# Squares of six blocks added by accumulating DMAs before TensorE sums them over the channels

## The chip, the cores and the metric

The kernel runs on one core of one Trainium2 chip. The metric is the device time of one execution in microseconds (us). Before the change it is 4678.69 us, the median of three runs (4672.37 to 4686.97).

## The reference, cut to what matters

Two layers work on x of shape (4, 1024, 1024). Each first forms a two-sided decayed sum over the sequence from the side tensor and gates it (`_bi_wkv`). The first layer ends in a linear map; the second ends in a root-mean-square norm, a router with top-4 of 32 experts, the experts, and a shared expert. The part that the change touches is the norm:

```python
def _rmsnorm(x, w, eps=EPS):
    var = jnp.mean(jnp.square(x.astype(jnp.float32)), axis=-1, keepdims=True)
    return (x * lax.rsqrt(var + eps)).astype(x.dtype) * w
...
h = _rmsnorm(x, norm_w)
flat = h.reshape(-1, H)
```

The mean of squares goes over the 1024 channels of each token.

## The kernel before, in words

Activations lie channel by channel: 128 channels on the partitions, tokens along the free axis. So there are CB = 8 blocks of 128 channels, and the 4096 tokens are worked on in HALVES = 8 halves of HALF = 512 tokens.

The program has three stages. In the first (units 0 to 7, up to about 330 us) VectorE (DVE), ScalarE (ACT) and GpSimd (POOL) compute the decayed sums of the first eight units alone, while TensorE (PE) helps to split weights. In the second (about 330 to 2000 us) each half has 32 steps. A step on PE is one `product` (L1457): 24 matmuls of 128x512. Steps 0 to 15 are the linear map of this half (`STEP_L`) and the shared expert's down product of the half before (`STEP_D`); steps 16 to 31 are gate and up products. Beside them halves 0 to 5 compute four more units each (`unit`, eight `fill` calls a unit, so that unit number q of a half holds fills 8q to 8q+7); halves 6 and 7 have no units. In the third stage (from about 2000 us) the experts are worked through.

All engines are programmed in order, by hand. Each engine's code for step i of half h is its `fill(h, i, ...)`; PE's is in `half`. The tables at the head of the file say at which step something is done. What the change touches, all in the second stage:

- DVE forms `C1[o]` (L1291), the normed layer's input, block o = 0 to 7.
- ACT squares it into the tile `SQ` at fill `SQUARE_AT[o]` = 3, 4, 5, 7, 9, 11, 13, 13 (L785). `SQ` is one buffer, so each square waits until the one before has been summed (semaphore `sums`).
- PE adds each square over the channels by one float32 matmul with the matrix `ones` (L1467, `square_sums`) after step `SUM_AT[o]` = 5, 5, 6, 8, 10, 12, 13, 14, accumulating in `SUM_BANK`. The trace shows each as two records.
- At step 15 (`R_AT`) ACT takes Ln and Exp of the sum into the tile `R` (L793, L795); DVE refines it (`root`, L1253 to L1261) and scales the blocks with it (`normalize`, L1270). PE then turns them by token (`by_token`, L1477, L1479), which waits for DVE.

Around them on ACT: at the fills of a unit, `edges` (L680, L683) copies the last column of a forward scan, which DVE's backward scan (L975, L983) starts from; `euk`, `inverse` and `sigmoid` (L652 to L656) also feed DVE. In unit q = 0 of a half, square 1 (fill 4) stands on ACT directly ahead of `edges(1)`, behind the issue of the side tensor's load (L665). `out_copy` (L768) copies turned outputs of the half before into the tile `RS`, and waits for the last store from it, which SP issues (L468) behind its loads of weight pieces (L396), which wait for PE's products.

POOL has one instruction for each unit, `clip` (L595), which waits for the side tensor's load and gives ACT's `side_exp` its input. From half 6 on it writes the experts' lists.

Of the kernel before, what the change touches and what calls it, by code (L numbers as in the profile page):

```python
# [9 lines left out]
CB = CH // P  # L10
TOK = BATCH * SEQ
TT = TOK // P
BLOCKS = BATCH * CB
HALF = SEQ // 2
HT = HALF // P
HALVES = TOK // HALF
PIECE = CB * P
FILLS_PER_UNIT = 8
UNITS_PER_HALF = BLOCKS // HALVES
STEPS = FILLS_PER_UNIT * UNITS_PER_HALF  # L20

ROUTED_TILES = TOK * TOPK // P + EXPERTS
# [18 lines left out]
SQUARE_AT = (3, 4, 5, 7, 9, 11, 13, 13)  # L41
SUM_AT = (5, 5, 6, 8, 10, 12, 13, 14)
R_AT = 2 * CB - 1

# [46 lines left out]
def adaln_moe(nc, x_t, side_t, cond, w_all, u_all, lin_sb, norm_w, router_t, shared_w, expert_w, out):  # L91
# [12 lines left out]
    with ctx:  # L104
# [76 lines left out]
        ones = sb("ones", P)  # L181
# [21 lines left out]
        s = {}  # L203
        for name in (
            "k_in x_in ramp consts_in cond_in kc ek ekv euk h_fwd h_edge h_bwd h_all den g_ln g_inv nf n_edge nb "
            "wv_done num num_w newton1 newton2 sig_steps sig_x gated gated_raw ratio ratio_out gated_out "
            "split_hi split_lo split_pe chunk product read_out c_hi c_lo sig1_steps sig1 c1 z sq z_hi z_lo res "
            "z_tr logits sums z_copy z_out mean r_ln r_exp newton_r r_set l_copy l_tr l_acc silu_steps silu_sig "
            "a_hi_s a_lo_s o_tr o_copy o_out prep prep_act masks rt rt_act rt_mask rt_pe cnt_copy "
            "fill_set fill_out add_idx_set apart entry_ready listed_in slots_in cols_set w1_hi w1_lo w2_hi w2_lo w1_read w2_read "  # L210
            "rows_in row_idx_set x_tr x_hi x_lo silu_done act_done a_tr a_hi a_lo y_hi y_lo y_out zero_set "
            "zero_out"
        ).split():
            s[name] = sem(name)
# [39 lines left out]
        def final(h, which=HALVES - 1):  # L254
            return isinstance(h, int) and h == which


# [275 lines left out]
        def _(pool):  # L533
# [56 lines left out]
            def clip(u, par):  # L590
# [4 lines left out]
                pool.tensor_scalar(EK, side_of[par], 30.0, None, ALU.min).then_inc(s["kc"], 1)  # L595

            clip(0, 0)
            with pool.Fori(0, BLOCKS // 2) as v:
                clip(2 * v + 1, 1)
                clip(2 * v + 2, 0)  # L600
            pool.wait_ge(s["zero_set"], 1)
            pool.dma_start(out[TOK:TOK + P, :], SPARE).then_inc(s["y_out"], 16)
            pool.wait_ge(s["rt_mask"], 1)
            pool.iota(entry.rearrange("p (t k w) -> p t k w", k=TOPK, w=2)[:, :, :, 0],
# [35 lines left out]
        def _(sc):  # L640
# [134 lines left out]
            def fill(h, i, first, prev, next_):  # L775
                if prev and i == 0:
                    act_hi(h - 1, CB - 1)
                if not before_all(h):
                    for o in range(CB):
                        if prev and i == copy_step(o):  # L780
                            out_copy(h - 1, o)
                        if i == square_step(o):
                            sc.wait_ge(s["c1"], h * CB + (o + 1))
                            wait(sc, "sums", h * CB + o)
                            sc.activation(SQ, C1[o], ACT.Square).then_inc(s["sq"], 1)  # L785
                    for o in range(CB):
# [4 lines left out]
                    if i == R_AT:  # L791
                        sc.wait_ge(s["sums"], h * CB + CB)
                        sc.activation(R, SUM_BANK, ACT.Ln, bias=eps[:, :], scale=1.0 / CH).then_inc(s["r_ln"], 1)  # L793
# [617 lines left out]
        def _(pe):  # L1411
# [49 lines left out]
            def square_sums(h, o):  # L1461
                pe.wait_ge(s["sq"], h * CB + (o + 1))
                if o == 0:
                    wait(pe, "z_copy", h * CB)
                    if final(h):
                        pe.wait_ge(s["entry_ready"], 1)
                pe.matmul(SUM_BANK, ones[:, :], SQ, start=(o == 0), stop=(o == CB - 1)).then_inc(s["sums"], 1)  # L1467

# [218 lines left out]
```

## Time and profile before

| | before |
|---|---|
| median of the runs | 4678.69 us |
| profiled execution, its span | 4682.9 us |
| PE busy | 4475.7 us, 96% |
| DVE busy | 2567.2 us, 55% |
| ACT busy | 1789.8 us, 38% |
| POOL busy | 722.8 us, 15% |
| time before the experts (first two stages) | about 2000 us |

The profiled execution has no time of its own listed beside its span; the span is 4.2 us above the median and within the range of the runs. Busy time is the time in which an engine works on an instruction; shares are of the span. A number in brackets behind a timeline row is how long the engine stood idle before it, and what ended that.

### The profile page before, as it was taken

What the parts mean: (1) busy time and instruction counts of PE and PEld (TensorE: products, weight loads), DVE (VectorE), ACT (ScalarE), POOL (GpSimd) and SP (SyncE); (2) the same over time, 40 slices, a digit from 0 to 9 for tenths busy, and PEclk for the clock granted to TensorE, in tenths of its full rate; (3) what the DMA queues carried; (4) which work ended last, traced back from release to release, by engine and by line L of the source; (5) the groups of instructions that cost most, each with busy time, mean ns of one, the idle gap of its engine ahead of it and who ended that gap; (6) DMA issues with size and microseconds to landing.
All of it is one profiled execution on the core that took longest, in us unless ns stands there. A gap on an engine that the chain in (4) does not pass through costs nothing.

```text
span 4682.9 us, 60901 instructions
## 1 busy us (share of the span) xinstructions
PE 4475.7 (96%) x19862; PEld 3545.7 (76%) x19863; DVE 2567.2 (55%) x2765; ACT 1789.8 (38%) x2596; POOL 722.8 (15%) x934
## 2 busy tenths in 40 slices
PE   6777999999999999999999999999999999999998
PEld 2245877777777877878888888888888888888887
DVE  8999999999999653433233434444341253333432
ACT  5665555555555333232222323334231142222321
POOL 1000000000000017211111112112111121111111
PEclk8888999999999999999999999999999999999999
DMA  6675767767676766754344545555552254444543
GB/s 226 235 263 184 274 241 268 251 223 282 240 268 226 270 212 190 251 182 111 95 131 112 170 112 160 171 166 150 182 168 57 61 186 145 112 112 116 161 109 61
DMA packets 247928, 835.08 MB, mean 178 GB/s; under 512 B 28160, under 2 KB 61056, under 8 KB 222976
## 3 DMA queue, kind: packets, MB, share of 16 engines
q1 hardware_dynamic: 172944, 572.77, 34.5%
q0 software_dynamic: 47728, 160.07, 15.5%
q10 hardware_dynamic: 27136, 100.67, 5.8%
q8 instruction: 72, 1.18, 0.1%
q14 instruction: 48, 0.39, 0.0%
HBM read 652.40 MB, written 181.01 MB: 178 GB/s over the span
## 4 chain that ended last, share of the span: by engine, by line
PE 80%; DVE 10%; issue 4%; ACT 3%; DMA 2%; POOL 0%; ACTq 0%; DVEq 0%; POOLq 0%; SPq 0%
PE ps L1593 34%; PE ps L1457 22%; PE ps L1607 16%; PE ps L1526 3%; PE ps L1479 1%; PE ps L1582 1%; DVE work L969 1%; DVE work L975 1%; DMA work<-rows_dram,row_idx 1%; PE ps L1477 1%; PE ps L1467 1%; DVE work L996 1%; DVE work L998 1%; DVE work L972 1%; DVE work L1002 1%
## 5 line engine op out<-in xcount | busy, mean ns | idle before, releaser
L1593 PE MATMUL ps<-halves 128*128 128x512 f32 x7152 | 1698.6, 393 | 3.5 <-DVE halves L1356 2.8
L1593 PEld LDWEIGHTS ps<-halves 128*128 128x128 f32 x7152 | 1338.5, 189 | 279.9 <-DVE halves L1356 3.1
L1457 PE MATMUL ps<-halves 128*128 128x512 f32 x6144 | 1450.2, 395 | 13.7 <-issue 12.5
L1457 PEld LDWEIGHTS ps<-halves 128*128 128x128 f32 x6144 | 1154.1, 189 | 287.2 <-issue 47.8
L1607 PE MATMUL ps<-halves 128*128 128x512 f32 x3576 | 834.9, 389 | 1.3 <-DVE halves L1372 1.3
L1607 PEld LDWEIGHTS ps<-halves 128*128 128x128 f32 x3576 | 671.1, 188 | 140.9 <-DVE halves L1372 1.6
L1356 DVE TENSOR_TENSOR halves<-ps,halves 128x1024 fp32r<-128x1024 f32 x150 | 183.7, 1225 | 905.2 <-ACT halves L852 905.2
L1351 DVE TENSOR_TENSOR halves<-work,halves 128x1024 fp32r<-128x1024 f32 (+1 forms) x320 | 440.2, 1433 | 83.6 <-ACT halves L856 83.3
L852 ACT ACTIVATE halves<-ps 128x1024 fp32r<-128x1024 f32 x150 | 154.0, 1027 | 862.4 <-PE ps L1593 862.4
L576 POOL DMA_INDIRECT out<-work,add_idx x149 | 249.8, 1677 | 1417.3 <-DVE work L1378 1382.2
L856 ACT ACTIVATE halves<-work 128x1024 fp32r<-128x1024 f32 (+1 forms) x320 | 369.1, 1229 | 67.0 <-PE ps L1607 56.5
L1372 DVE TENSOR_TENSOR halves<-ps,halves 128x256 fp32r<-128x256 f32 x298 | 112.4, 419 | 491.7 <-ACT halves L884 491.7
L595 POOL TENSOR_SCALAR work<-work 128x1024 f32<-128x1024 f32 x33 | 106.5, 3226 | 1419.9 <-DMA work<-side_t 1419.9
L884 ACT ACTIVATE halves<-ps 128x256 fp32r<-128x256 f32 x298 | 98.5, 382 | 544.4 <-PE ps L1582 544.4
L1378 DVE TENSOR_SCALAR work<-ps,acc 128x512 f32<-128x512 f32 x149 | 111.6, 749 | 276.4 <-PE ps L1607 266.5
L890 ACT ACTIVATE work<-ps,acc 128x512 f32<-128x512 f32 x149 | 102.1, 685 | 408.5 <-PE ps L1607 388.5
L566 POOL DMA_INDIRECT work<-rows_dram,row_idx x151 | 152.5, 1010 | 123.4 <-POOL row_idx L562 69.0
L1526 PE MATMUL ps<-ident,work 128*128 128x128 f32 x1200 | 157.6, 275 | 12.4 <-DMA work<-rows_dram,row_idx 12.4
L975 DVE TENSOR_TENSOR_SCAN work<-decay,edge_in,work 128x1024 f32<-128x1024 f32 x64 | 154.2, 2409 | 14.2 <-ACT edge_in L680 14.2
L1435 PE MATMUL ps<-plain,ident 128*128 128x512 f32 x128 | 83.0, 736 | 73.6 <-ACT halves L735 73.6
L983 DVE TENSOR_TENSOR_SCAN work<-decay,edge_in,work 128x1024 f32<-128x1024 f32 x64 | 150.7, 2355 | 0.0
L1526 PEld LDWEIGHTS ps<-ident,work 128*128 128x128 f32 x1200 | 137.1, 142 | 13.4 <-DMA work<-rows_dram,row_idx 13.3
(186 smaller groups left out, 3674.4 us busy)
## 6 DMA issues: line engine op xcount, KB each, us to landing
halves<-split_dram SPq DMA_DIRECT2D x512, 512.0 KB, 5.6
work<-expert_w SPq DMA_DIRECT2D x192, 1024.0 KB, 5.5
split_dram<-halves ACTq DMA_DIRECT2D x32, 1024.0 KB, 4.9
plain<-shared_w SPq DMA_DIRECT2D x32, 512.0 KB, 3.2
gated_dram<-work ACTq DMA_DIRECT2D x32, 512.0 KB, 4.1
work<-side_t ACTq DMA_DIRECT2D x32, 512.0 KB, 5.6
work<-x_t ACTq DMA_DIRECT2D x32, 512.0 KB, 3.7
ratio_dram<-work ACTq DMA_DIRECT2D x32, 512.0 KB, 4.2
```

The costliest lines, as they stand in the source:

```text
L566: pool.indirect_dma_start(hx, None, rows_dram[:, :], bass.IndirectOffsetOnAxis(row_idx[:, :].bitcast(u32), 0)).then_inc(s["rows_in"], 16)
L576: pool.indirect_dma_start(out[:, :], bass.IndirectOffsetOnAxis(add_idx[:, :].bitcast(u32), 0), y, None, compute_op=ALU.add).then_inc(s["y_ ...
L852: sc.activation(xhi, ps_xt[:, :], ACT.Copy).then_inc(s["x_hi"], 1)
L856: sc.activation(whi[q][:, part], staged(q, part), ACT.Copy).then_inc(s["w1_hi" if q < 4 else "w2_hi"], 1)
L975: ve.tensor_tensor_scan(F[:, ::-1], d, F[:, ::-1], edge_in[:, 0:1], ALU.mult, ALU.add).then_inc(s["h_bwd"], 1)
L983: ve.tensor_tensor_scan(G[:, ::-1], d, G[:, ::-1], edge_in[:, 1:2], ALU.mult, ALU.add).then_inc(s["nb"], 1)
L1351: ve.tensor_tensor(wlo[q][:, part], staged(q, part), whi[q][:, part].bitcast(f32), ALU.subtract)\
L1356: ve.tensor_tensor(xlo, ps_xt[:, :], xhi.bitcast(f32), ALU.subtract).then_inc(s["x_lo"], 1)
L1457: last = pe.matmul(bank(k % 4), w, op[:, part], start=(c == 0 and w is w_hi and op is hi), stop=(c == CB - 1 and w is w_lo))
L1526: last = pe.transpose(ps_xt[:, c * P:(c + 1) * P], hx[:, c * P:(c + 1) * P], ident[:, :])
L1593: last = pe.matmul(ps_h[:, a * 512:a * 512 + 512], xp[:, xk * P:(xk + 1) * P], wp[:, rhs], start=(xk == 0 and xp is xhi and wp is whi[q]), ...
L1607: last = pe.matmul(ps_y[:, h * 512:h * 512 + 512], ap_[:, (q * 2 + k) * P:(q * 2 + k + 1) * P], wp[:, rhs:rhs + 512], start=(q == 0 and k ...
```

## The change

In halves 0 to 6 only block 0's square goes to another tile, `R`, which is free at that time. The squares of blocks 1 to 5 still go to `SQ`, and each is added to `R` by a DMA with an accumulate, which POOL issues (`fold_square`): SBUF to SBUF, 128 partitions of 2 KB. So ACT's square o (2 to 6) waits for the landing of DMA o-1 (semaphore `sq_folded`) in place of a matmul. PE sums `R` once, at o = 5 (after step 12), then squares 6 and 7: three matmuls with `ones` in place of eight. Half 7 is as before. POOL's loop over the units is written out from unit 8 on, with the DMAs between the clips.

```diff
+ALONE = 2 * UNITS_PER_HALF
...
+FOLDED = 6
...
+        def folded(h):
+
+            return not final(h)
+
+        def squares_used(h, o):
+
+            return h * (CB - FOLDED + 1) + (o + 1 if final(h) else o - FOLDED + 2)
...
+            def fold_square(h, o):
+
+                pool.wait_ge(s["sq"], h * CB + (o + 1))
+                pool.dma_start(R, SQ, accum_op=ALU.add).then_inc(s["sq_folded"], 16)
+
             clip(0, 0)
-            with pool.Fori(0, BLOCKS // 2) as v:
+            with pool.Fori(0, ALONE // 2) as v:
                 clip(2 * v + 1, 1)
                 clip(2 * v + 2, 0)
+            for h in range(HALVES - 2):
+                for q in range(UNITS_PER_HALF):
+                    u = ALONE + h * UNITS_PER_HALF + q
+                    if q == 0:
+                        fold_square(h, 1)
+                    if q == 1:
+                        fold_square(h, 4)
+                        fold_square(h, 5)
+                    clip(u + 1, (u + 1) % 2)
+                    if q == 0:
+                        fold_square(h, 2)
+                        fold_square(h, 3)
             pool.wait_ge(s["zero_set"], 1)
             pool.dma_start(out[TOK:TOK + P, :], SPARE).then_inc(s["y_out"], 16)
+            for o in range(1, FOLDED):
+                fold_square(HALVES - 2, o)
...
                             sc.wait_ge(s["c1"], h * CB + (o + 1))
-                            wait(sc, "sums", h * CB + o)
-                            sc.activation(SQ, C1[o], ACT.Square).then_inc(s["sq"], 1)
+                            if folded(h) and o == 0:
+                                wait(sc, "z", h * CB)
+                            elif folded(h) and o <= FOLDED:
+                                wait(sc, "sq_folded", 16 * (h * (FOLDED - 1) + (o - 1)))
+                            else:
+                                wait(sc, "sums", squares_used(h, o - 1))
+                            sc.activation(R if folded(h) and o == 0 else SQ, C1[o], ACT.Square).then_inc(s["sq"], 1)
...
             def square_sums(h, o):
-                pe.wait_ge(s["sq"], h * CB + (o + 1))
-                if o == 0:
+                first = FOLDED - 1 if folded(h) else 0
+                if o < first:
+                    return
+                if o == first:
                     wait(pe, "z_copy", h * CB)
                     if final(h):
                         pe.wait_ge(s["entry_ready"], 1)
-                pe.matmul(SUM_BANK, ones[:, :], SQ, start=(o == 0), stop=(o == CB - 1)).then_inc(s["sums"], 1)
+                if folded(h) and o == first:
+                    pe.wait_ge(s["sq_folded"], 16 * ((h + 1) * (FOLDED - 1)))
+                else:
+                    pe.wait_ge(s["sq"], h * CB + (o + 1))
+                pe.matmul(SUM_BANK, ones[:, :], R if folded(h) and o == first else SQ, start=(o == first), stop=(o == CB - 1))\
+                    .then_inc(s["sums"], 1)
```

PE, in the loop over the halves, at the end of steps 5 and 6. Before:

```order
L1457 MATMUL ps<-halves 128x512 x11
L1467 MATMUL ps<-work,ones 128x512 [waits z_copy,sq]
L1490 REGISTER_ALU
L1493 MATMUL ps<-ident,work 128x128 [waits o_copy,read_out]
L1493 MATMUL ps<-ident,work 128x128 x3
L1467 MATMUL ps<-work,ones 128x512 [waits sq]
L238 REGISTER_ALU
L1457 MATMUL ps<-halves 128x512 [waits piece_in2_0,read_out]
```

Now (the changed file's L1491 is the product, L1534 the turning of outputs):

```order
L1491 MATMUL ps<-halves 128x512 x11
L1531 REGISTER_ALU
L1534 MATMUL ps<-ident,work 128x128 [waits o_copy,read_out]
L1534 MATMUL ps<-ident,work 128x128 x3
L240 REGISTER_ALU
L1491 MATMUL ps<-halves 128x512 [waits piece_in2_0,read_out]
```

Two sums and their waits for a square are gone here; the first sum now stands behind step 12 and waits for `sq_folded`.

ACT, in half 2, around fill 4 of its first unit (q = 0). Before:

```order
L665 DMA work<-side_t 128x1024 [waits gated]
L785 ACTIVATE work<-plain 128x512 [waits sums,c1]
L680 ACTIVATE edge_in<-work,edge 128x1 [waits h_fwd]
L683 ACTIVATE edge_in<-work,edge 128x1 [waits nf]
L691 ACTIVATE work<-work,uu 128x1024 [waits gated_raw]
L785 ACTIVATE work<-plain 128x512 [waits sums,c1]
```

Now:

```order
L694 DMA work<-side_t 128x1024 [waits gated]
L819 ACTIVATE work<-plain 128x512 [waits sq_folded,c1]
L709 ACTIVATE edge_in<-work,edge 128x1 [waits h_fwd]
L712 ACTIVATE edge_in<-work,edge 128x1 [waits nf]
L720 ACTIVATE work<-work,uu 128x1024 [waits gated_raw]
L819 ACTIVATE work<-plain 128x512 [waits sq_folded,c1]
```

The order is the same. The first of the two squares (block 1) now waits for the last DMA of the half before; the second (block 2) waits for the DMA of block 1.

POOL, in one half (h = 0 to 5) of the changed kernel, where before there were only the four clips (L605 now, L595 before):

```order
L610 DMA work<-work 128x512 [waits sq]
L605 TENSOR_SCALAR work<-work 128x1024 [waits ekv,k_in,h_fwd]
L610 DMA work<-work 128x512 [waits sq] x4
L605 TENSOR_SCALAR work<-work 128x1024 [waits ekv,k_in,h_fwd] x3
```

The DMA of block 1 stands ahead of the clip of unit q = 0; those of blocks 2 and 3 behind it, and those of blocks 4 and 5 ahead of the clip of unit q = 1.

## Rows read from the trace of the kernel before

**Rows 1.** The page, span in 40 slices: busy tenths of PE and DVE

```profile
PE   6777999999999999999999999999999999999998
DVE  8999999999999653433233434444341253333432
```

**Rows 2.** Windows: span; busy us (instructions) of PE, PEld, DVE, ACT, POOL; PEclk, DMA, GB/s

```profile
330.90:538.60 207.70, 172.22 (x695) 129.05 (x694) 198.69 (x174) 113.35 (x158) 15.15 (x4) 0.89 0.61 219
746.40:955.60 209.20, 202.14 (x870) 156.63 (x869) 195.30 (x173) 114.94 (x163) 13.38 (x5) 0.98 0.73 257
1575.90:1779.70 203.80, 200.60 (x874) 155.74 (x873) 97.34 (x154) 61.46 (x100) 34.58 (x36) 0.99 0.67 221
```

**Rows 3.** Waits of PE and DVE, 538.6 to 1440 us: total us, times, longest

```profile
PE ps L1457 <- issue: 12.5, 5, 3.1
PE ps L1477 <- DVE work L1270: 11.2, 5, 3.1
DVE work L975 <- ACT edge_in L680: 14.2, 8, 5.1
DVE work L1270 <- PE ps L1479: 6.4, 16, 1.5
```

**Rows 4.** Timeline of PE, half 2: start us, us, engine, instructions [idle before <-releaser]

```profile
748.33 1.12 PE L1467 MATMUL ps<-work,ones 128*128 128x512 f32 x2 [0.34 <-ACT work L785]
...
754.79 1.02 PE L1467 MATMUL ps<-work,ones 128*128 128x512 f32 x2
755.24 6.05 PE L1457 MATMUL ps<-halves 128*128 128x512 f32 x24
761.13 0.60 PE L1493 MATMUL ps<-ident,work 128*128 128x128 f32 x4
761.49 5.70 PE L1457 MATMUL ps<-halves 128*128 128x512 f32 x24
767.03 1.02 PE L1467 MATMUL ps<-work,ones 128*128 128x512 f32 x2
```

**Rows 5.** Timeline of ACT, half 3: square 1, ahead of the edge copy

```profile
956.87 0.63 ACT L785 ACTIVATE work<-plain 128x512 f32<-128x512 f32 x1 [13.30 <-PE ps L1467]
```

**Rows 6.** Timeline of DVE: the scan that waits for it, halves 2 to 5

```profile
748.57 2.35 DVE L975 TENSOR_TENSOR_SCAN work<-decay,edge_in,work 128x1024 f32<-128x1024 f32 x1 [2.19 <-ACT edge_in L680]
957.79 2.35 DVE L975 TENSOR_TENSOR_SCAN work<-decay,edge_in,work 128x1024 f32<-128x1024 f32 x1 [5.12 <-ACT edge_in L680]
1164.69 2.35 DVE L975 TENSOR_TENSOR_SCAN work<-decay,edge_in,work 128x1024 f32<-128x1024 f32 x1 [3.58 <-ACT edge_in L680]
1372.89 2.35 DVE L975 TENSOR_TENSOR_SCAN work<-decay,edge_in,work 128x1024 f32<-128x1024 f32 x1 [1.94 <-ACT edge_in L680]
```

**Rows 7.** Timeline of SP, half 6: store of an output block, behind the loads

```profile
1634.72 0.43 SPq L468 DMA_DIRECT2D out<-work  x1
```

**Rows 8.** DMA issues: engine, op, count, median us from issue to landing

```profile
rows_dram<-plain SPq DMA_DIRECT2D x8, 2048.0 KB, 9.2
out<-work SPq DMA_DIRECT2D x64, 256.0 KB, 5.5
out<-work,add_idx POOLq DMA_INDIRECT x149, 6.3
slots_dram<-acc POOLq DMA_INDIRECT x128, 3.7
```

**Rows 9.** The page, costly groups: busy, mean ns of one

```profile
L576 POOL DMA_INDIRECT out<-work,add_idx x149 | 249.8, 1677 | 1417.3 <-DVE work L1378 1382.2
```

**Rows 10.** Timelines of ACT and DVE, half 2: squares 4, 5 and who needs them

```profile
775.60 0.61 ACT L785 ACTIVATE work<-plain 128x512 f32<-128x512 f32 x1
782.05 0.62 ACT L785 ACTIVATE work<-plain 128x512 f32<-128x512 f32 x1
784.08 0.63 ACT L656 ACTIVATE work<-work 128x512 f32<-128x512 f32 x1
787.14 0.69 DVE L1291 TENSOR_TENSOR plain<-work 128x512 f32<-128x512 f32 x1
```

More of the change, by code:

```diff
@@ L207, in adaln_moe @@
             "split_hi split_lo split_pe chunk product read_out c_hi c_lo sig1_steps sig1 c1 z sq z_hi z_lo res "
-            "z_tr logits sums z_copy z_out mean r_ln r_exp newton_r r_set l_copy l_tr l_acc silu_steps silu_sig "
+            "z_tr logits sums sq_folded z_copy z_out mean r_ln r_exp newton_r r_set l_copy l_tr l_acc silu_steps silu_sig "
             "a_hi_s a_lo_s o_tr o_copy o_out prep prep_act masks rt rt_act rt_mask rt_pe cnt_copy "
@@ L791, in fill @@
                     if i == R_AT:
-                        sc.wait_ge(s["sums"], h * CB + CB)
+                        sc.wait_ge(s["sums"], squares_used(h, CB - 1))
                         sc.activation(R, SUM_BANK, ACT.Ln, bias=eps[:, :], scale=1.0 / CH).then_inc(s["r_ln"], 1)
```

## The prediction, made before the changed kernel ran

> **What bounds the kernel now.** The slices of the page come first [rows 1]: up to about 1640 us DVE is at 9 tenths in nearly every slice and PE too; from there PE alone is. So before one counts PE's time as the kernel's, one must know who leads in the halves. The windows, cut at each half's first sum, show it [rows 2]: in half 2 PE is busy 202.1 of 209.2 us and DVE 195.3; in half 0 DVE is busy 198.7 of 207.7 and PE only 172.2; in half 6, without units, DVE works 97.3 and PE 200.6 of 203.8. The waits tell who follows whom [rows 3]. Between the first sum of half 1 and the norm of half 5, PE stands idle 12.5 us at loop boundaries and 11.2 us in front of the transposes of z, for DVE. DVE hardly ever waits for a product. Its two largest waits on others are 14.2 us for ACT's `edge_in` and 6.4 us inside the norm, for the logits. I read this as: **DVE leads from half 0 to the norm of half 5; after that PE does**, in the rest of half 5 and in half 6. The granted clock is 0.98 and 0.99 in the windows of halves 2 and 6, so nearly no time can come from the clock.
>
> DVE's wait for `edge_in` is tied to the squares. ACT's square of block 1 waits for PE's first sum, because `SQ` is one buffer: it waited 13.30 us in half 3 [rows 5], and with it all that stands behind it on ACT, first the edge copies. So DVE's scan L975 begins late, by 2.19, 5.12, 3.58 and 1.94 us in halves 2 to 5 [rows 6]: 12.8 us together, which is most of the 14.2 us [rows 3]. Half 1 has no such gap; DVE is still too late there for ACT to hold it up.
>
> **What the change removes from PE.** The time of one sum, from the starts [rows 4]: from a sum over the next product to the transposes, 754.79 to 761.13, is 6.34 us; a product alone, 761.49 to 767.03, is 5.54. So a sum takes **0.80 us**, and 7 halves x 5 sums = 35 sums are 28.0 us of PE time. The wait of the second sum for its square, 0.34 us in halves 1 to 6 [rows 4], goes too: 2.0 us. PE has 30 us less to do. What of it lies on the path:
>
> - Half 0: DVE leads, and no gap of its scans there hangs on a sum. I count 0.
> - Halves 1 to 5, up to the norm of half 5: PE would come earlier to places where it waits for DVE in any case. PE's own gain is hidden; it only makes those waits longer. I count 0 for the matmuls.
> - Half 6: PE leads. 5 x 0.80 + 0.34 = **4.3 us**. What ends the stretch is the norm, behind ACT's copy of an output, which waits for the store of the one before. SP issues that store at 1634.72, right when step 14 of PE has ended [rows 7]; it is paced by PE and moves with it. So all 4.3 us count.
>
> **What it removes from ACT's waits.** Square 1 now waits for a DMA of the half before, and square 0 for the z of the half before; both are long done. The edge copies follow at once, and the scans of halves 2 to 5 start without the gap: **12.8 us** on DVE, which leads there. In half 3 the removed gap (5.12) is more than PE's saving before the norm (4.34), so some tenths could come back as a wait; I leave that to the range.
>
> **What it adds.** 35 DMAs of 256 KB, 5 in a half. No accumulating DMA from SBUF to SBUF is in this trace, so its time from the end of a square to the landing, L, must be bounded. Short end: a small POOL DMA lands in 3.7 us [rows 8]; with at least 1 us to issue that is 4.7. Long end: the largest landing here is 9.2 us, for 2 MB [rows 8]; with the 1.68 us that an accumulating indirect DMA takes POOL [rows 9], 10.9. Nearest rows: stores of the same 256 KB in the same stage land in 5.5 us, and accumulating DMAs of 512 KB in 6.3 [rows 8]. I take **L = 1 + 5.5 = 6.5 us**.
>
> Who waits for it? ACT's next square. The tightest pair that feeds something is squares 4 and 5 [rows 10]: the first ends at 776.21, the second starts at 782.05, 5.84 us later. A landing after 6.5 us holds ACT 0.7 us. Behind it stands a sigmoid that ends at 784.71, and DVE takes its result at 787.14; so ACT may be 2.43 us late before DVE loses anything. **Up to L = 8.3 us the DMA costs nothing.** Squares 1 and 2, and 2 and 3, have no less room by the order of ACT's work: square 1 now comes right after the load of the side tensor is issued, and the edge copies, which wait for two scans of DVE, stand between it and square 2. If DVE's schedule slid, the price would be L - 8.3 at each of three places, in six halves. The first sum on PE, after step 12, needs all five DMAs: PE may wait there a us or two, but in halves 0 to 5 it follows DVE anyhow, and in half 6, where ACT has no units to serve, square 5 comes early in its step.
>
> On POOL each DMA delays what is behind it by its 1 to 1.7 us, and waits for a square. Behind the DMA of block 1 and behind those of blocks 4 and 5 stands a clip; its input arrives later than those squares, so the clip is not held. The DMAs of blocks 2 and 3 stand behind a clip, which costs them up to its 3 us; that is inside the room above. POOL's later work, the lists, waits for DVE. The extra 9 MB go to DMA engines whose share in these windows is 0.61 to 0.73 [rows 2], so there is room for them.
>
> In this stage DVE is busy nearly all the time that POOL issues these DMAs. The accumulating indirect DMAs of the third stage take POOL 1.68 us beside a DVE at 3 to 4 tenths [rows 1, 9]; no row shows a DMA of POOL beside a DVE at 9 tenths. A rule of the Trainium skill speaks against the change here: the page "SBUF — State Buffer", section "Who interferes with whom", says that a VectorE instruction in a 2-port mode (copy, cast, tensor_scalar) locks GpSimd out of the shared ports, and an issue of a DMA needs them; the same page gives some 0.62 us that become 3.1. As an estimate by that page L would be 6.5 + 2.5 = 9.0 us, and the three places would cost 3 x 0.7 x 6 = 13 us, most of the gain. DVE's instructions around the squares are scans and tensor_tensor [rows 6, 10], which that section does not count among the locking ones for writes of descriptors. I keep 6.5.
>
> **The sum:** 12.8 + 4.3 = 17.1 us, nothing added. The profiled span of 4682.9 becomes 4665.8. It stands 4.2 above the median, and the comparison is with the median: 4678.7 - 17.1 = **4661.6 us**, 0.37% faster. What a measurement of this kernel can tell from no change is about 0.3%, 14.0 us, which is close to my gain.
>
> **The rivals.**
>
> *PE leads after all* (chance 0.12). If DVE's full look in halves 1 to 5 came from following PE, all 30 us less on PE would count: 4649. For: PE is busy 97% of half 2 [rows 2]. Against: PE's waits for DVE, 12.5 + 11.2 = 23.7 us [rows 3], and a DVE that never waits for products.
>
> *The wait comes back* (0.26). DVE's gap at the scan goes, but ACT is then held at square 2 or 5, or PE's later arrival at the out copies and stores takes over, so that halves 1 to 5 keep their length. Left is half 6: 4678.7 - 4.3 = 4674. For: L is unknown, DVE may be kept from or keep POOL from its ports, and ACT's chain of copies and stores has a landing of 5.5 us between two copies [rows 8]. Against: the 2.4 us of room.
>
> *The DMAs land late* (0.13, the other side). One mechanism: ACT waits for `sq_folded` at squares 2, 3 and 5 in halves 0 to 5, and DVE runs dry behind it. It decides from L = 8.3 + 17.1/18 = 9.3 us on. At the long end of 10.9 the price is 3 x 2.6 x 6 = 47 us, less 17: up to 4709; with more room at squares 2 and 3 than at 5, rather 4698. By the lock rule of the Trainium skill's "SBUF — State Buffer" the time would be 4661.6 + 13 = 4675 (an estimate); that outcome lies among those of the second rival and in its chance.
>
> That the change does not do what it says I give nothing: the listing has three sums for eight in each half up to 6, and the DMAs in POOL's stream.
>
> **How the numbers follow.** The forecast, a gain of 12 to 22 us, has 0.49; of that some 0.35 lies beyond 14 us. With the first rival that makes 0.47 for faster by over 0.3%. Within: the rest of the forecast and the second rival, with a little of the third, 0.41. Slower by over 0.3%: 0.12. The range goes from the PE-led case, 4648, over the forecast and the returned wait to 4684, where late DMAs begin to cost; it leaves out the rest of that rival and a stronger gain.
>
> **What would show it.** Right: sums on PE 29 x 2 records for 64 x 2; no gap of 2 us or more before the scan L975 in the first unit of halves 2 to 5; half 6 shorter by 4 us; PE's waits for z in halves 1 to 5 longer than before (each by about 2 us); landing from POOL about 5 to 6 us, ACT's wait for it under 1 us each. Wrong: halves 1 to 5 each shorter by over 4 us (PE led), or DVE waiting for ACT's sigmoid behind squares 2, 3 and 5 (late DMAs), or DVE waits of the same total at another line (the wait came back).

## The result, and the profile after

The changed kernel takes 4684.53 us (median; 4677.61 to 4695.72), against 4678.77 us for the kernel before in the same job. The ratio is 1.0017, with a 95% interval of 1.001 to 1.0024: slower by 0.1 to 0.24%, where 0.37% faster was forecast. The profiled execution took 4690.1 us with a span of 4688.2, against the span of 4682.9 before; its mean granted clock is 0.976, against 0.979.

**Where the time went.** The start of DVE's first `normalize` of each half (the norm) cuts both traces at the same place of the program. The page's slices answer to [rows 1] and look alike, since DVE and PE stay full:

```profile
PE   6786999999999999999999999999999999999998
...
DVE  8999989999899753333233434444341152333432
```

The windows show the difference. Their columns are: window, length, then busy us (instructions) of PE, PEld, DVE, ACT and POOL, then PEclk, DMA share and GB/s. Of the kernel before, from the norm of half 0 to that of half 5 (five halves with units), and from there to the norm of half 6 (called half 6):

```profile
403.10:1439.20 1036.10, 1005.57 (x4336) 779.50 (x4336) 975.98 (x864) 573.99 (x813) 64.89 (x20) 0.99 0.72 253
1439.20:1643.60 204.40, 201.16 (x868) 155.98 (x868) 152.41 (x162) 88.49 (x131) 6.60 (x3) 0.98 0.71 244
```

The same of the changed kernel:

```profile
403.40:1453.30 1049.90, 993.88 (x4286) 772.88 (x4286) 976.43 (x865) 574.09 (x813) 91.14 (x45) 0.98 0.75 256
1453.30:1651.20 197.90, 195.12 (x858) 153.70 (x858) 152.42 (x161) 88.39 (x131) 11.18 (x8) 0.99 0.75 258
```

The five halves with units grew by 13.8 us; half 6 shrank by 6.5; the rest of the program differs by -2.0. The sum is the 5.3 us between the spans. PE was busy 11.7 us less in the five halves, where 25 sums of 0.80 us fewer would make 20. DVE did the same work. Both stood idle longer: DVE 73.5 us in place of 60.1, PE 56.0 in place of 30.5. (By single halves, from norm to norm: 6.3, 3.4, -1.3, 3.8 and 1.6 us longer.)

The waits of the changed kernel between the first sum of half 1 and the norm of half 5 answer to [rows 3]; in each row the total us, the times, the longest:

```profile
ACT work L797 <- DMA out<-work: 123.7, 19, 10.1
...
DVE work L1009 <- ACT edge_in L709: 23.8, 9, 4.5
...
PE ps L1507 <- DMA work<-work: 16.8, 5, 3.9
ACT work L819 <- DMA work<-work: 12.8, 5, 3.1
```

Before, the same stretch had these rows, the first of them for the same wait:

```profile
ACT work L768 <- DMA out<-work: 88.6, 19, 7.7
...
ACT work L785 <- PE ps L1467: 73.7, 10, 13.3
```

The wait of square 1 for a sum (in the second row, 13.3 us in half 3 [rows 5]) is gone, as meant. But DVE's scan waits 23.8 us for the edge copy, 14.2 before [rows 3]. The timelines of half 2 say where. ACT's, around square 1 and then around the third out copy:

```profile
748.90 0.63 ACT L819 ACTIVATE work<-plain 128x512 f32<-128x512 f32 x1 [3.81 <-DVE work L1041]
752.11 0.30 ACT L709 ACTIVATE edge_in<-work,edge 128x1 f32<-128x1 f32 x1 [2.58 <-DVE work L1003]
...
758.75 0.63 ACT L819 ACTIVATE work<-plain 128x512 f32<-128x512 f32 x1 [3.12 <-DMA work<-work]
...
788.41 0.62 ACT L819 ACTIVATE work<-plain 128x512 f32<-128x512 f32 x1
...
801.24 0.60 ACT L797 ACTIVATE work<-ps 128x512 f32<-128x512 f32 x1 [10.08 <-DMA out<-work]
...
803.78 0.28 ACT L709 ACTIVATE edge_in<-work,edge 128x1 f32<-128x1 f32 x1
```

DVE's scans behind those two edge copies (the first answers to [rows 6]: its gap has gone):

```profile
754.09 3.06 DVE L1009 TENSOR_TENSOR_SCAN work<-decay,edge_in,work 128x1024 f32<-128x1024 f32 x1
...
804.16 2.59 DVE L1009 TENSOR_TENSOR_SCAN work<-decay,edge_in,work 128x1024 f32<-128x1024 f32 x1 [4.51 <-ACT edge_in L709]
```

And what SP, POOL and PE did meanwhile:

```profile
789.01 0.43 SPq L478 DMA_DIRECT2D out<-work  x1
...
789.33 0.86 POOL L610 DMA_DIRECT2D work<-work  x1 [5.61 <-ACT work L819]
...
798.85 2.08 PE L1507 MATMUL ps<-work,ones 128*128 128x512 f32 x2 [3.62 <-DMA work<-work]
```

SP issues the store of out copy 2 at 789.01; the DMA of block 5 follows 0.3 us later, 6.5 us behind that of block 4. Out copy 3 starts when the store has landed, at 801.24, which is **12.2 us** after the issue. In the kernel before the same pair reads

```profile
782.21 0.43 SPq L468 DMA_DIRECT2D out<-work  x1
...
790.46 0.60 ACT L768 ACTIVATE work<-ps 128x512 f32<-128x512 f32 x1 [5.75 <-DMA out<-work]
```

which is 8.2 us. Behind out copy 3 stand three ACT steps and the edge copy of the unit q = 1, and DVE's scan, which lost 2.19 us in the first unit of this half, now loses 4.51 in the second. PE waits for the last of the DMAs too, 3.62 us, and the wait costs more than its length. The sum behind it took 2.08 us, where a sum without such a wait took 1.02, and the product behind that one 6.91, where it took 6.05 [rows 4]. The granted clock was 0.83 and 0.82 in the windows 795 to 800 and 800 to 805, and 1.00 in those beside them, so for a part of them PE ran at the lower of its two levels, 1.2 and not 2.4 GHz:

```profile
799.94 6.91 PE L1491 MATMUL ps<-halves 128*128 128x512 f32 x24
...
800.00:805.00 5.00, 5.00 (x19) 3.71 (x18) 0.84 (x1) 3.69 (x7) 1.43 (x1) 0.82 0.94 370
```

The chain of waits over the five halves agrees, by line, from its heaviest entry on. Before:

```profile
by line: PE ps L1457 52.6%; issue 7.9%; PE ps L1479 4.0%; DVE work L969 3.0%; DVE work L975 2.8%; PE ps L1477 2.5%; PE ps L1467 2.4%; DVE halves L1239 2.3%; DVE work L983 1.5%; DVE work L998 1.4%; DVE work L996 1.4%; DVE work L979 1.3%; DVE
```

After:

```profile
by line: issue 26.5%; PE ps L1491 23.2%; DMA out<-work 8.1%; DMA work<-work 6.2%; PE ps L1520 4.3%; DMA work<-side_t 2.6%; PE ps L1518 2.6%; DVE work L1003 1.7%; POOL work L605 1.6%; DVE halves L1273 1.3%; ACT work L683 1.3%; DVE work L1009
```

Two things are to be seen. Before, over half of the chain is PE's product, in a stage that the prediction gave to DVE. After, transfers have come in: the stores and the accumulating DMAs hold 14%. The smaller share of PE's product is not to be read: five times the chain runs through POOL's idle time ahead of the first DMA of a half (41.6 us in one piece in half 2, listed as "issue"), while PE and DVE work. What can be read is where the chain goes at the end of each unit stretch. In halves 1 and 3 it goes through the last DMA to PE's sum, in halves 2, 4 and 5 through the store to out copy 3:

```profile
577.90 9.54 DMA work<-work
...
789.01 12.15 DMA out<-work
...
997.29 9.30 DMA work<-work
...
1205.87 12.13 DMA out<-work
...
1417.12 11.85 DMA out<-work
```

### The profile page after: what moved, and what is told of

Same layout as the page of the kernel before. It is cut to its first block, busy times and chain, and to the rows that moved or that the text cites. A ratio compares the mean times of both kernels' runs of the same rounds, so it can differ in the third digit from the quotient of the medians.

```text
span 4688.2 us, 60740 instructions
## 1 busy us (share of the span) xinstructions
PE 4448.4 (95%) x19790; PEld 3532.6 (75%) x19793; DVE 2568.0 (55%) x2765; ACT 1789.8 (38%) x2596; POOL 761.4 (16%) x969
## 4 chain that ended last, share of the span: by engine, by line
PE 72%; issue 9%; DVE 8%; DMA 6%; ACT 4%; POOL 1%; SPq 0%; ACTq 0%; DVEq 0%; POOLq 0%
PE ps L1634 33%; PE ps L1648 16%; PE ps L1491 15%; PE ps L1567 3%; DMA out<-work 2%; DMA work<-work 2%; PE ps L1520 2%; PE ps L1623 1%; DMA work<-rows_dram,row_idx 1%; PE ps L1518 1%; DVE work L1003 1%; DMA work<-side_t 1%; DVE work L1030 1%; DVE work L1006 1%; DVE work L1032 1%
## 5 line engine op out<-in xcount | busy, mean ns | idle before, releaser
L1491 PE MATMUL ps<-halves 128*128 128x512 f32 x6144 | 1435.3, 394 | 12.3 <-issue 11.4
L1491 PEld LDWEIGHTS ps<-halves 128*128 128x128 f32 x6144 | 1153.7, 189 | 274.3 <-issue 35.0
L605 POOL TENSOR_SCALAR work<-work 128x1024 f32<-128x1024 f32 x33 | 110.8, 3357 | 985.8 <-DMA work<-side_t 985.8
L1009 DVE TENSOR_TENSOR_SCAN work<-decay,edge_in,work 128x1024 f32<-128x1024 f32 x64 | 157.4, 2459 | 23.8 <-ACT edge_in L709 23.8
```

The lines of the kernel that those rows point to most:

```text
L1009: ve.tensor_tensor_scan(F[:, ::-1], d, F[:, ::-1], edge_in[:, 0:1], ALU.mult, ALU.add).then_inc(s["h_bwd"], 1)
L1491: last = pe.matmul(bank(k % 4), w, op[:, part], start=(c == 0 and w is w_hi and op is hi), stop=(c == CB - 1 and w is w_lo))
```

## The experiments

The changed kernel's slow place can be the store of an out copy (the new load of DMAs makes it late), ACT's squares (each waits for a landing), or PE's first sum (it waits for the last landing). The runs take the parts apart. "Stretch" is the time from the norm of half 0 to that of half 5; its DVE busy time is 975 to 978 us in all kernels where nothing else is said. On the chip of the first four that are told below (no DMAs, idle DMAs, two buffers, three blocks) the kernel before took 4811.2 us, and half 7 took 330 to 332 us in their profiles (203.5 in the profile of before), in that of two buffers with PE's granted clock at 0.50 for 120 us of it; for them ratios and stretches are compared, not times. Each stretch is that of one profiled execution.

| kernel | stretch | PE busy in it | half 6 | ratio to before [95%] |
|---|---|---|---|---|
| before | 1036.1 | 1005.6 | 204.4 | 1 |
| changed | 1049.9 | 993.9 | 197.9 | 1.0017 [1.001, 1.0024] |
| changed, again | 1044.8 | 994.8 | 197.0 | 1.0012 [1.0002, 1.0022] |
| no DMAs | 1019.8 | 982.0 | 198.2 | 0.9966 [0.9953, 0.9978] |
| before, with idle DMAs | 1048.5 | 1010.6 | 203.3 | 1.0032 [1.0018, 1.0047] |
| before, with two buffers | 1033.4 | 1002.7 | 202.5 | 0.9992 [0.9983, 1.0002] |
| DMAs 1 to 3, sum after step 8 | 1049.4 | 1001.7 | 198.7 | 1.0027 [1.0017, 1.0036] |
| DMAs 1 to 3, sum after step 10 | 1026.4 | 995.5 | 199.8 | 0.9972 [0.9961, 0.9984] |
| the same, again | 1023.0 | 994.6 | 200.0 | 0.9978 [0.9969, 0.9987] |
| five DMAs, sum after step 13 | 1058.7 | 996.7 | 198.1 | 1.0025 [1.0016, 1.0035] |
| three sums, only DMAs 1 to 3 | 1022.0 | 985.1 | 198.2 | 0.9968 [0.9955, 0.998] |
| three sums, only DMAs 4 and 5 | 1044.7 | 994.0 | 196.9 | 1.0005 [0.9995, 1.0014] |
| POOL adds all five | 1036.0 | 987.7 | 198.2 | 1.0003 [0.9993, 1.0013] |
| DMAs 1 to 3, POOL adds 4 and 5 | 1040.7 | 993.3 | 198.0 | 0.9996 [0.9986, 1.0006] |

**No DMAs.** The changed kernel, with a semaphore increment where each DMA was. It leaves out the squares of blocks 1 to 5.

```diff
-                pool.dma_start(R, SQ, accum_op=ALU.add).then_inc(s["sq_folded"], 16)
+                pool.sem_inc(s["sq_folded"], 16)
```

> The changed kernel without its accumulating DMAs: POOL only passes the semaphore on, so the squares of blocks 1 to 5 are formed and not added. Measured so far from the first norm to that of half 5: 1036.1 us before, 1049.9 changed. Theory A (contention: the DMAs fall into a stretch in which the DMA engines are full, and make the store that ACT's out copy waits for late): with the DMAs gone DVE loses neither the old gap at its scan nor the new one; this stretch takes about 1023 us and the kernel 4660. Theory B (pace: PE without its sums reaches its products earlier, so SP issues piece loads earlier, ahead of the same store, DMAs or not): the new gap of 4.5 us a half stays, the stretch takes 1040 to 1050 us and the kernel 4675 to 4683.

The stretch is 1019.8 us, 16.3 shorter than before and 25 to 30 shorter than with the DMAs; ratio 0.9966. So the saving was there to be had, and the DMAs cost more than it. The waits, as above:

```profile
ACT work L797 <- DMA out<-work: 89.9, 19, 8.0
...
DVE work L1009 <- ACT edge_in L709: 1.4, 3, 0.7
```

Without the DMAs the out copies wait as before (88.6), and DVE's gaps at the scan are gone. PE runs the same 4286 records of the stretch as in the changed kernel, but is busy with them 982.0 us and not 993.9: of the 30.1 us between these two profiles 11.9 are PE's slower matmuls and 18.2 its idle time.

**Before, with idle DMAs.** The kernel before, and five DMAs a half at the same places, which add `C1[0]` to `R`. They serve nothing; ACT waits for them only where it writes `R`.

```diff
+            def idle_fold(h, o):
+                pool.wait_ge(s["sq"], h * CB + (o + 1))
...
+                pool.dma_start(R, C1[0], accum_op=ALU.add).then_inc(s["sq_folded"], 16)
```

> The kernel before with 25 to 30 accumulating DMAs of 256 KB issued by POOL at the places of the change (halves 0 to 5, five each, block C1[0] onto the tile R, which is cleared first and is not read before it is overwritten); all eight sums stay on PE, and squares wait as before. Theory A: the DMAs alone delay the store; first norm to that of half 5 rises from 1036 to 1045 to 1052 us, kernel 4688 to 4695. Theory B: PE's pace is the old one, so the stretch stays within 3 us of 1036 and the kernel at 4679 to 4682.

Nobody waits for these DMAs at a square or a sum, and still the stretch grows by 12.4 us, and the whole by 0.32%, as theory A had it:

```profile
ACT work L791 <- DMA out<-work: 112.0, 19, 9.8
...
ACT work L808 <- PE ps L1491: 69.0, 10, 11.8
...
DVE work L999 <- ACT edge_in L703: 26.4, 13, 4.2
```

DVE's wait for the edge copy rose by 12.2 us over that of before, nearly the whole growth of the stretch. So the mere presence of the transfers costs this much, and the longer waits are the out copies'.

**Before, with two buffers.** Only the wait of square 1 is taken away: the squares go to `R` and `SQ` in turn, and PE makes all eight sums.

```diff
+        SQS = [R, SQ]
...
+                            if o:
+                                wait(sc, "sums", h * CB + o - 1)
+                            sc.activation(SQS[o % 2], C1[o], ACT.Square).then_inc(s["sq"], 1)
...
+                pe.matmul(SUM_BANK, ones[:, :], SQS[o % 2], start=(o == 0), stop=(o == CB - 1)).then_inc(s["sums"], 1)
```

> The kernel before with one edit: the squares alternate between the tiles R and SQ, so that square 1 need not wait for the sum of square 0; no DMAs, eight sums on PE. Theory A: DVE leads, its gap of 12.8 us at the scan in halves 2 to 5 goes and nothing replaces it: first norm to that of half 5 about 1023 us, kernel about 4666. Theory B says nothing against this, since PE keeps its work. Theory C (the chain of out copies and stores takes over whenever DVE comes earlier): the stretch stays at about 1036 and the kernel at 4678.

The stretch is 1033.4 us: 2.7 us less, not 12.8. The ratio, 0.9992 with an interval from 0.9983, leaves at most 8 us for the whole kernel. The gaps at the scan are gone (0.4 us left), and DVE waits for PE's product instead, at a line where the kernel before had 1.1 us in this stretch:

```profile
DVE work L1252 <- PE ps L1461: 6.7, 4, 2.8
```

Against "no DMAs" the five sums a half are worth 1033.4 - 1019.8 = 13.6 us more. **Taking away the wait alone is worth little, with the sums it is 16.3**: DVE and PE are both close to the lead. (The sums were not taken away alone.)

**Three blocks.** The changed kernel with `FOLDED = 4`: DMAs of blocks 1 to 3 only, five sums in place of eight, the first of them after step 8. The calls for blocks 4 and 5 are taken out of POOL's stream; of the edit only this line is shown.

```diff
-FOLDED = 6
+FOLDED = 4
```

> The changed kernel with FOLDED = 4: only the squares of blocks 1 to 3 are added by DMAs, all in the first unit of a half, and PE does five sums (blocks 0 to 3 together, then 4 to 7). Theory A: the two DMAs next to the late store are gone, so the new gap shrinks to 1 us or less; first norm to that of half 5 about 1025 to 1030 us, half 6 shorter by 2.5 us, kernel 4666 to 4672. Theory B: PE is still 2.5 us earlier at that place, the gap stays at 2.5 us or more: stretch 1040 us, kernel about 4680.

A miss for both theories: the stretch is 1049.4, as long as with five DMAs, but with other waits. PE's first waits in it, and DVE's:

```profile
PE ps L1504 <- DMA work<-work: 13.9, 5, 3.5
```

```profile
DVE work L1279 <- PE ps L1488: 18.9, 7, 3.4
```

The first sum stands too close behind the third DMA. PE waits for the landing, all its later work is late, and DVE waits for PE's products. Hardly a gap is left at the scan (1.2 us).

**The changed kernel again**, on the chip of the runs that follow:

> The changed kernel once more, as the mark for the others on this chip: ratio 1.0017 to before, first norm to that of half 5 about 1050 us (before 1036), half 6 about 198 (before 204).

Ratio 1.0012, stretch 1044.8 where the first profile had 1049.9. So a profiled stretch of one kernel can differ by 5 us, and smaller differences in the table are not read.

**Three blocks, sum after step 10.** As "three blocks", with the first sum two steps later.

```diff
+FOLDED_SUM_AT = (5, 5, 6, 10, 10, 12, 13, 14)
...
-                        if i == sum_step(o):
+                        if i == (FOLDED_SUM_AT[o] if folded(h) else sum_step(o)):
```

> Blocks 1 to 3 added by DMAs (as e4_three_blocks), but PE's first sum stands after step 10 in place of step 8. If the time of e4_three_blocks came from PE standing 2.2 to 3.6 us at that sum for the landing of the third DMA, and DVE then waiting for PE (3.4 and 2.1 us in half 4), the stretch from the first norm to that of half 5 falls from 1049 to about 1030 us, and the ratio from 1.0027 to 0.998. If the three DMAs cost by contention in the unit q = 0 itself, the stretch stays above 1042.

The stretch is 1026.4 us and the ratio 0.9972: PE waits for no DMA, DVE's gaps at the scan are 3.7 us in all. One number in a table turns 0.27% slower into 0.28% faster, and the stretch is 23.0 us shorter, though PE had waited only 13.9 us for the DMA: PE is also busy 6.2 us less with the same 4306 records. Run again on another chip, with more executions:

> e8_late_sum_three once more in more rounds, as the version that computes everything and beats both kernels: ratio 0.997 to 0.998 to before; first norm to that of half 5 about 1026 us, half 6 about 200. If the gain of e8_late_sum_three was chance, the ratio lies above 0.999.

4667.01 us against 4678.41, ratio 0.9978 [0.9969, 0.9987], stretch 1023.0. **This version computes everything and is faster than both kernels**, than the one before by 11 us. In the chain of waits over the stretch PE's product holds the lead again (55.7%), and among the waits stand

```profile
ACT work L795 <- DMA out<-work: 92.5, 19, 9.1
...
DVE work L1007 <- ACT edge_in L707: 3.6, 6, 1.1
```

**Five DMAs, sum after step 13.** The same remedy for the changed kernel: `FOLDED_SUM_AT = (5, 5, 6, 8, 10, 13, 13, 14)`.

> The changed kernel with PE's first sum after step 13 in place of step 12, so that PE need not stand there 2.3 to 3.6 us for the last DMA. Theory A (the late store and DVE's gap of 4.2 to 4.5 us behind it decide): PE's wait goes, the gap stays, the stretch stays at 1046 to 1050 us, ratio 1.001. Rival (PE's wait for the landing decides): the stretch falls by 2.5 to 3.5 us a half, to 1035, ratio 0.9985.

A miss: 1058.7 us, ratio 1.0025. The wait for the DMA has gone from PE's rows, but DVE's gap stays (21.7 us), and new waits stand at the turning of an output block and at DVE's next use of a product:

```profile
PE ps L1535 <- DVE work L1283: 29.0, 5, 7.0
...
DVE work L1283 <- PE ps L1492: 12.4, 5, 2.6
```

Behind step 13 the two sums stand behind that turning, which waits for DVE, and ACT's square 7 waits for them (31.0 us in five halves, 19.3 in the changed kernel). So this edit puts a longer wait of PE, 29.0 us, in place of the 16.8 for the DMA, and PE's matmuls were slower behind it too (a record of the sum took 902 ns in the mean, 592 or 593 in the kernels where PE does not wait there). It shows that the gap at the scan does not hang on PE's wait for the DMA. How much of the changed kernel's loss is that wait it can't tell, nor is it settled beyond these rows why the total is 9 to 14 us over the changed kernel.

**Which DMAs?** Three sums a half as in the changed kernel, but in halves 0 to 5 only the DMAs of blocks 1 to 3, or only those of 4 and 5, are issued. Both leave the squares of the other blocks out. Shown is the main line of the first; the second has `4 <= o <= 5` there.

```diff
-                pool.dma_start(R, SQ, accum_op=ALU.add).then_inc(s["sq_folded"], 16)
+                if h == HALVES - 2 or 1 <= o <= 3:
+                    pool.dma_start(R, SQ, accum_op=ALU.add).then_inc(s["sq_folded"], 16)
```

> The changed kernel, in halves 0 to 5 with the DMAs of blocks 1 to 3 alone: the squares of blocks 4 and 5 are formed and not added; half 6 has all five. PE sums three times, as in the change. Theory A (the DMAs of blocks 4 and 5 are the ones that hurt, by the late store and by PE's wait for the last landing): DVE's gap of 4.2 to 4.5 us and PE's wait go; first norm to that of half 5 from 1050 to 1022 to 1028 us, ratio 0.995 to 0.997. Rival (the landing of 7.8 us at square 2 costs as much as the rest): the stretch stays above 1036.

> The counterpart: in halves 0 to 5 the DMAs of blocks 4 and 5 alone, the squares of blocks 1 to 3 are formed and not added. Theory A: gap of 4.2 to 4.5 us at DVE's scan and PE's wait of 2.3 to 4.0 us at its first sum stay; stretch 1043 to 1050 us, ratio 1.000 to 1.0015. Rival: the stretch falls by half of the 30 us between the change and the kernel without DMAs, to 1035 or less, ratio 0.9985 or less.

Over the 1019.8 us without any, DMAs 1 to 3 cost 2.2 us, DMAs 4 and 5 cost **24.9** (by the ratios 1 and 18 us of the whole kernel). With the first three alone ACT waits 12.4 us in front of squares, as in the changed kernel (12.8), and it costs next to nothing. With the last two alone:

```profile
ACT work L804 <- DMA out<-work: 108.0, 19, 9.5
...
DVE work L1017 <- ACT edge_in L716: 16.9, 5, 4.3
PE ps L1516 <- DMA work<-work: 15.9, 5, 3.9
```

Both waits are back, in all five halves. This places the cost: it comes with the two transfers that fall beside the store of out copy 2 and stand right ahead of PE's first sum. It does not divide the cost between these two. The presence of idle transfers alone cost 12.4 us; as an estimate from that, and if the parts add, PE's wait and its slower matmuls hold the other 13 to 18 of the 25 to 30 us.

**POOL adds instead.** The same sums formed by POOL's own instruction, no DMA.

```diff
-                pool.dma_start(R, SQ, accum_op=ALU.add).then_inc(s["sq_folded"], 16)
+                pool.tensor_tensor(R, R, SQ, ALU.add).then_inc(s["sq_folded"], 16)
```

> The changed kernel with each accumulating DMA replaced by an add of the same tiles on POOL itself (tensor_tensor, 128x512 float32); all is computed. Contention theory (A): no DMA is added, so out copies and PE's first sum wait for nothing new; POOL's reads can hold a DVE instruction with two SBUF inputs by 0.8 us, as the clips do, at most 4 us a half. First norm to that of half 5 between 1020 and 1037 us, half 6 at 198, kernel 6 to 22 us below before (ratio 0.995 to 0.999). A rival (any addition outside PE comes too late): PE waits at its first sum for sq_folded by over 2 us a half as with the DMAs, stretch 1045 or more, ratio 1.001 or more.

1036.0 us, ratio 1.0003: the stretch lies at the edge of its range, the ratio is a miss. The out copies wait as before (88.7 us), but DVE works longer: 994.2 us in the stretch, 18 more than before, and that takes back what the DMAs' absence gave.

```profile
405.30:1441.30 1036.00, 987.74 (x4286) 772.44 (x4286) 994.19 (x865) 576.30 (x813) 132.55 (x45) 0.98 0.71 253
```

**Three DMAs, two adds.** Blocks 1 to 3 by DMA, 4 and 5 by POOL's add.

```diff
+                if h == HALVES - 2 or 1 <= o <= 3:
+                    pool.dma_start(R, SQ, accum_op=ALU.add).then_inc(s["sq_folded"], 16)
+                else:
+                    pool.tensor_tensor(R, R, SQ, ALU.add).then_inc(s["sq_added"], 1)
```

> The changed kernel with the squares of blocks 1 to 3 added by DMAs and those of blocks 4 and 5 by POOL itself (all is computed; three sums on PE in halves 0 to 6). Theory A: no gap at the scan behind the store, no wait of PE for a landing, and POOL's two adds hold DVE by 1 to 2 us a half (five adds cost it 3.8 us a half in e9_pool_adds): stretch 1028 to 1035 us, half 6 at 198, ratio 0.996 to 0.998. Rival as for e11_only_dmas_1_3: stretch above 1040, ratio 1.000.

1040.7 us, ratio 0.9996: also a miss. DVE is busy 9 us more, PE waits 11.1 us for DVE at the turning of an output, and the out copies wait 107.1 us though no DMA falls beside the store of out copy 2. Why, was not tried.

## Why the prediction was wrong

**Two steps failed.** The forecast lost its gain by the term "nothing added": the DMAs were priced at 0 and cost 25 to 30 us in the stretch. And the reading of who leads was wrong, so that what is removed came out right by luck.

**Who leads.** The prediction read DVE as the leader of halves 0 to 5 and counted PE's matmuls there as 0 and the gap of the scans in full. The runs show two engines nearly level, so its first rival, in which PE leads, was half true. The wait of square 1 taken away alone gave 2.7 us, not 12.8 (both by single profiles, good to 5 us); the sums then gave 13.6 more, of the 25 x 0.80 = 20 us that PE has less to do in the stretch. Together that is 16.3 us, close to 12.8 by luck. The evidence stood in the profile before: the chain of waits has PE's product at 52.6% of this stretch, and the prediction never read it. That DVE "hardly ever waits for a product" was taken as a sign that PE had slack; it only says that DVE's gaps at the scans had so far been at least as long as PE's lateness.

**The sum of 17.1 us was nearly right for what is removed.** The kernel without the DMAs has 16.3 us less in the stretch and 6.2 in half 6 by its profile, and by the runs a ratio of 0.9966, which is 16.4 us on that chip. What turned it round is the term "nothing added", in the two places told below.

**Half 6** shrank by 6.5 us, not 4.3. The mechanism is right: 197 to 200 us in all kernels with three or five sums, 202.5 to 204.4 in the three with eight. Two buffers alone took 1.9 us, but the kernel with idle DMAs, whose half 6 is the old one, also took 1.1 less than before; so whether the waits between a sum and its square were worth more than the 0.34 is not shown. From two buffers to no DMAs the five sums gave 4.3.

**The gap at the scan, first unit:** right. The scan starts at 754.09 without a gap. PE's waits for the z, which were to grow by about 2 us in each half, went only from 23.1 to 24.8 us in all.

**L, the time to the landing:** undersized, and still not what cost the time. From the end of square 1 to the start of square 2 it was 758.75 - 749.53 = 9.2 us, where 6.5 were taken and 10.9 was the far bound. The view of the source line says, with the issue's duration in ns and the landing behind it in us (least, median, most):

```profile
L610 POOL DMA_DIRECT2D work<-work x35: 860/869/953, 337.7 to 1614.6; - x35
...
DMA to landing us min/median/max: 3.3/7.8/10.1
```

That is 0.9 + 7.8 = 8.7 us. The limit worked out for it, 8.3 us, was thought to decide; the kernel with DMAs 1 to 3 has nearly the same landing (7.5 us in the median) and the same wait of ACT in front of squares, and loses 2.2 us. So the third rival, ACT held at the squares, is refuted as the cause, although its sign came true.

**"PE may wait there a us or two, but in halves 0 to 5 it follows DVE anyhow":** false in both parts. It waits 2.3 to 3.9 us in each half, 16.8 in five. Behind the wait the granted clock is lower, which the prediction did not count ("nearly no time can come from the clock"): a record of the sum took 774 ns in the mean, and 593 in the kernel without DMAs. With only three DMAs, moving the sum from step 8 to step 10 took 23.0 us off the stretch, which with the wait had been as long as the changed kernel's.

**"There is room for them":** this is the other place. The share of 0.61 to 0.73 [rows 2] is a mean over 200 us. Windows of 5 us around the store of out copy 2 in half 2 of the changed kernel show what the mean hides:

```profile
780.00:785.00 5.00, 5.00 (x24) 4.13 (x23) 5.00 (x5) 4.90 (x7) 0.86 (x1) 1.00 1.03 373
785.00:790.00 5.00, 5.00 (x26) 4.16 (x25) 5.00 (x7) 4.80 (x7) 0.68 (x1) 1.00 0.53 147
790.00:795.00 5.00, 5.00 (x24) 3.99 (x22) 4.90 (x6) 1.13 (x2) 0.19 (x1) 1.00 0.87 239
795.00:800.00 5.00, 1.38 (x5) 0.63 (x3) 4.66 (x3) 0.00 (x0) 0.00 (x0) 0.83 1.06 366
```

The engines were full already behind the store in the kernel before (1.00 and 1.03 in the windows 785 to 790 and 790 to 795). A transfer put there delays a store whose landing ACT, then the edge copy, then DVE wait for. The kernel with idle DMAs lost 12.4 us by this path alone.

**The second rival** ("the wait comes back") named the right form: the out copies and stores take over. Its price, 4674, was a return to the old length; in truth the new wait is longer than the old one (23.8 us for 14.2), and the chance of 0.26 was too small for a mechanism whose chain the prediction had itself written down.

**The lock rule** was no step of the sum, and no run here tests it. By the Trainium skill, page "SBUF — State Buffer", section "Who interferes with whom", what keeps GpSimd from the writes that an issue of a DMA needs is a VectorE instruction in a 2-port mode (copy, cast, tensor_scalar). In the five halves of the changed kernel DVE ran ten copies and tensor_scalars in 976 us, all others were scans, tensor_tensor and scalar_tensor_tensor. POOL's issue took 0.86 to 0.95 us beside a DVE busy 93% of the time. The time to the landing grew all the same: L came out at 8.7 us, close to the 9.0 that the prediction had estimated by that page. Whether a part of it has to do with DVE, or all of it with the full DMA engines, stays open.

## What to carry to other kernels

When two engines are both busy over 90% of a stage, read the chain of waits of that stage as well as the waits, and price a saving by what the other engine allows; a removal on one side alone may give a fifth of its size. A new transfer is priced by the DMA share in the few us where it falls and by the transfer that somebody waits for there, not by the stage's mean; here three of five DMAs were nearly free and the other two cost all of the gain. A wait of PE is priced with the slower matmuls behind it. Put the first reader of an accumulating DMA well behind it: with three DMAs a half, two steps later on PE made 0.5% of difference.

## What the runs showed of the hardware

- **An accumulating DMA from SBUF to SBUF landed late here and took time of all DMA engines.** 256 KB landed in 7.8 us (median), 7.1 in the second profile, 6.1 with idle DMAs, where nobody but the next DMA waited for it. The page's row of its queue went from 160.07 MB and 15.5% of 16 engines' span to

```profile
q0 software_dynamic: 52768, 169.24, 16.7%
```

  so 35 DMAs took 0.167 x 4688.2 - 0.155 x 4682.9 = 57 us of all 16 engines, 1.6 us each (the shares are rounded, so 1.5 to 1.8). By the fit for software DMAs in the Trainium skill, page "DMA: Bandwidth & Descriptors", section "Anatomy of one DMA — SWDGE (gpsimd) path", 256 KB would take 2.6 us, an estimate; the median here is three times that, in a stage whose engines are busy three quarters of the time, and only the shortest landing, 3.3 us, comes near.
- **PE's matmuls were slower behind a wait of 3.4 to 3.9 us.** Both records of the first sum took 2.07 or 2.08 us together in the four halves with such a wait, in half 2 at a granted clock of 0.83 over 5 us; in half 4, with a wait of 2.35 us, they took 1.12.
- **POOL's add slows DVE beside it.** An add of 128x512 took POOL 1.43 us in the median (1.27 to 3.91), and DVE's busy time rose by 18 us for the 25 adds in the stretch, 0.7 us each. One of DVE's instructions of this kind, a scan of 2.3 us as a rule, ran from 1195.61 beside an add of POOL from 1195.26 to 1196.84, in the kernel with three DMAs and two adds:

```profile
1195.61 3.38 DVE L1030 TENSOR_TENSOR_SCAN work<-decay,edge_in,work 128x1024 f32<-128x1024 f32 x1
```
